# Third attention of a four-layer block: entry rebuilt, rows of the first batch first, differences on GpSimd

## The reference

```
k_raw, v_raw = context @ Wk.T, context @ Wv.T      # keys, values: odd and even columns of the pair
q = rmsnorm(layernorm(x) @ Wq.T)                   # 32 heads of 8, per head
k = rmsnorm(k)                                     # t * rsqrt(mean(t*t) + 1e-6) over the 8
out = softmax(q k / sqrt(8)) v                     # 256 queries, 1601 keys, per batch and head
x = x + out
```

## Time and profile before

| | |
|---|---|
| median of 3 runs | 2695.54 us (2695.38 to 2700.11) |
| the profiled execution | 2690.88 us |
| its span | 2689.1 us |
| TensorE busy, share of the span | 2465.2 us, 92% |
| VectorE | 1728.8 us, 64% |
| ScalarE | 1488.3 us, 55% |
| GpSimd | 1355.9 us, 50% |

### The profile page before, as it was taken

One profiled execution on the slowest core, in us unless ns is written; L12 is line 12 of the kernel. 1 busy time (PEld: TensorE's weight loads), 2 busy tenths in 40 slices (PEclk: granted clock), 3 DMA queues, 4 the chain that ended last, 5 costly groups with the idle time before them and its releaser, 6 DMA issues. The chain is left out here.

```text
span 2689.1 us, 53835 instructions
## 1 busy us (share of the span) xinstructions
PE 2465.2 (92%) x19554; PEld 1718.4 (64%) x19554; DVE 1728.8 (64%) x3372; ACT 1488.3 (55%) x3294; POOL 1355.9 (50%) x917
## 2 busy tenths in 40 slices
PE   6889999979999999999999999999599698989886
PEld 4567777746777777777777777777365343434443
DVE  4345667557877877877877787877213565555446
ACT  2235544445556566556566555565112577777895
POOL 0025655435666766666666666666101375757400
PEclk8889999999999999999999999999699799999999
DMA  4212232230001000010000000003201000000100
GB/s 157 78 54 83 89 94 73 71 123 1 16 17 45 17 17 9 9 45 16 17 17 16 30 17 17 17 1 126 102 10 58 19 20 15 20 15 20 50 4 16
DMA packets 42466, 108.77 MB, mean 40 GB/s; under 512 B 5044, under 2 KB 26040, under 8 KB 37048
## 3 DMA queue, kind: packets, MB, share of 16 engines
q1 hardware_dynamic: 40424, 102.41, 11.3%
q0 software_dynamic: 768, 2.10, 0.2%
q10 hardware_dynamic: 1008, 0.79, 0.1%
HBM read 99.91 MB, written 4.98 MB: 39 GB/s over the span
## 5 line engine op out<-in xcount | busy, mean ns | idle before, releaser
L1212 POOL TENSOR_TENSOR xn<-xn,l_p 128x512 f32<-128x512 f32 (+1 forms) x400 | 634.7, 1587 | 178.0 <-ACT l_p L1254 161.3
L2205 ACT ACTIVATE l_p<-psum 128x1024 f32<-128x1024 f32 x416 | 399.4, 1034 | 101.0 <-PE psum L2334 98.1
L1340 DVE TENSOR_TENSOR l_plo<-l_p,l_phi 128x512 fp32r<-128x512 f32 (+1 forms) x464 | 405.4, 875 | 63.1 <-ACT l_p L1254 41.1
L1253 ACT ACTIVATE l_phi<-psum 128x512 fp32r<-128x512 f32 (+1 forms) x464 | 279.4, 602 | 219.2 <-PE psum L447 139.8
L1389 DVE TENSOR_REDUCE l_mx<-psum 128x1 f32<-128x512 f32 (+2 forms) x512 | 306.2, 618 | 35.8 <-PE psum L1553 35.2
L2182 POOL TENSOR_TENSOR l_rs<-l_ms,half_power 128x32 f32<-128x32 f32 x45 | 247.5, 5500 | 122.8 <-DVE l_ms L2230 122.8
L2347 PE MATMUL psum<-l_p,l_vs 64*32 64x256 f32 x6656 | 260.5, 378 | 26.9 <-issue 21.6
L1254 ACT ACTIVATE l_p<-psum 128x512 f32<-128x512 f32 (+1 forms) x464 | 281.4, 606 | 0.0
L1483 PE MATMUL psum<-l_m,l_ones 128*128 128x512 f32 (+1 forms) x464 | 232.7, 502 | 0.0
L1572 PE MATMUL psum<-l_w,l_ctx 128*128 128x256 f32 (+1 forms) x832 | 217.0, 383 | 10.0 <-ACT l_qa L1271 6.2
L1553 PE MATMUL psum<-l_kThi,l_qThi 128*128 128x512 f32 (+2 forms) x512 | 199.4, 427 | 5.1 <-DVE l_mx L1389 2.3
(11 more groups left out here) (380 smaller groups left out, 5180.2 us busy)
## 6 DMA issues: line engine op xcount, KB each, us to landing
w_stage<-in_L_w_dram SPq DMA_DIRECT2D x76, 384.0 KB, 3.1
l_w<-in_L_w_qkv_dram SPq DMA_DIRECT2D x16, 1024.0 KB, 4.9
l_ct<-in_ctx_tiles_dram SPq DMA_DIRECT2D x52, 128.0 KB
c_T<-in_ctx_T_dram SPq DMA_DIRECT2D x4, 1601.0 KB
l_ctx<-in_ctx_T_dram SPq DMA_DIRECT2D x4, 1601.0 KB, 6.9
c_N<-in_ctx_dram SPq DMA_DIRECT2D x4, 1536.0 KB
s_wg<-in_L_gate_dram SPq DMA_DIRECT2D x4, 1024.0 KB, 11.8
s_wu<-in_L_up_dram SPq DMA_DIRECT2D x4, 1024.0 KB, 13.8
```

What stands on the lines that cost most here:

```text
L1212: g_.tensor_tensor(l2_acc[k][0:r, :], first[0:r, :], l2_p[c % 3][0:r, :], ALU.add)\
L1253: act.activation(l2_phi[c % 3][0:r, :], src, ACT.Exp).then_inc(l2_e, 1)
L1340: v.tensor_tensor(l2_plo[c % 3][0:r, :], l2_p[c % 3][0:r, :], l2_phi[c % 3][0:r, :].bitcast(F32), ALU.subtract)\
L2205: act.activation(l3_p[ring(odd, c)][:, :], psum[:, (c % 2) * 2 * BANK:(c % 2 + 1) * 2 * BANK], ACT.Exp, scale=float(D3) ** -0.5).then_inc( ...
```

## The change

Places. The entry goes through its 15 tiles in the order `ORDER` = key tiles 0 to 8, query tiles 0 and 1, key tiles 9 to 12; p is the place, QUERIES_AT = 9.

GpSimd. The low half's subtraction moves from VectorE to GpSimd (`low`), in the entry alone. Beside the first four of them GpSimd issues the eight gathers, two at a time; they are no longer in `top_pool`. Then come the inverse roots of rows 0 and 1, the other differences, the zeroing of `l3_vs[0]` after place 9, and behind the last difference `l3_vs[1]`, the copy into `l3_vs[0]`, the inverse roots of rows 2 to 7 and the memset of `l3_qT[1]`.

VectorE. Rows 0 and 1 are added and their statistics taken after place 3's pair, they are normalised after place 5's, rows 2 to 7 are added after place 7's. Statistics and normalising of rows 2 to 7 stand in steps 0 and 2 of batch 0, behind all of the entry. The scaled keys have two buffers (`l3_n`, `l3_sq`). TensorE turns rows 0 and 1 after the projection of place 7, ScalarE copies them before place 8's squares. Rows 2 to 7 are turned two at a time by TensorE at steps 5, 8 and 11 of batch 0 (`REST_TURN`), through bank 7, and copied by VectorE.

Copies. The first query tile is turned into bank 6 and copied by ScalarE at place 13, the second into bank 4 and copied by VectorE at the end.

Steps. The turn is at 15 + 6q instead of 14 + 6q, and VectorE's `turned` stands in the next step, behind `gather` and before `add_out` and `squares`. SyncE loads the query weights when the last expert tile is stored, before the loads of key tile 4 and on.

```diff
-            g.wait_ge(s_yland, 16 * TILES2)
-            for n in range(NT):
-                g.indirect_dma_start(s_yg[:, n, :], None, s_out[:, :], bass.IndirectOffsetOnAxis(s_pos[:, n:n + 1], 0))\
-                    .then_inc(s_got, 16)
...
+        def gather_rows(g, first, end):
+            for n in range(first, end):
+                g.indirect_dma_start(s_yg[:, n, :], None, s_out[:, :], bass.IndirectOffsetOnAxis(s_pos[:, n:n + 1], 0))\
+                    .then_inc(s_scat if n < TB else s_got, 16)
...
-        FIRST_HALF, SECOND_HALF, SQUARES, POWER, PAIRS, TURN = (beside(at) for at in (0, 3, 4, 5, 12, 14))
+        FIRST_HALF, SECOND_HALF, SQUARES, POWER, PAIRS, TURN = (beside(at) for at in (0, 3, 4, 5, 12, 15))
...
+        KEY_BANKS, TURN_BANKS, NORM_BANK, QUERY_BANK = (0, 1, 2, 3), (7, 5), 6, 4
+        ORDER = [*range(MC - PT), *range(MC, N3), *range(MC - PT, MC)]
+        QUERIES_AT = ORDER.index(MC)
+        COMBINE_AT, NORM_AT, REST_AT = 3, 5, 7
...
+            def queries(p):
+                act.wait_ge(l3_init, 1)
+                act.wait_ge(l3_T, p + 1)
+                for n in range(HG):
+                    dst, src = query_part(ORDER[p], n)
+                    ins = act.activation(dst, src, ACT.Copy)
+                ins.then_inc(l3_qd, 1)
...
+            for p in range(N3):
+                if p == QUERIES_AT - 1:
+                    act.wait_ge(xT_ps, LN_PS + 1)
+                    for c in range(DC):
+                        act.activation(xT[:, c, 0:S], bank(NORM_BANK, S, c * S), ACT.Copy).then_inc(xT_cp, 1)
+                square(p)
+                if ORDER[p] < MC:
+                    value(p)
+                if p >= 1:
+                    root(p - 1)
+                if p >= PT:
+                    turned(p - PT)
...
+            def pairs(p):
+                v.wait_ge(l3_rsd, p + 1)
+                need(v, l3_pd, p - 1)
+                need(v, l3_T, p - 1)
+                hi, _, norm, both = pair_parts(p)
+                dve_steps.then(v, v.tensor_tensor(norm, l3_heads(source(p)[:, 0:D]),
+                                                  l3_rs[p % PT][:, :].unsqueeze(2).to_broadcast([P, H3, D3]), ALU.mult))
+                v.tensor_copy(hi, both).then_inc(l3_hid, 1)
...
+                if p == COMBINE_AT + 1:
+                    combine(v, 0, TB)
+                    v.wait_ge(x_upd, X_AT[5] + TB)
+                    rows_stats(v, 0, TB)
+                if p == NORM_AT + 1:
+                    rows_norm(v, 0, 0, TB)
+                if p == REST_AT + 1:
+                    combine(v, TB, NT)
+            pairs(N3 - 1)
...
+            def low(p):
+                g.wait_ge(l3_hid, p + 1)
+                hi, lo, _, both = pair_parts(p)
+                g.tensor_tensor(lo, both, hi, ALU.subtract).then_inc(l3_pd, 1)
...
+            low(0)
+            g.wait_ge(s_yland, 16 * TILES2)
+            gather_rows(g, 0, TB)
+            low(1)
+            gather_rows(g, TB, TB + 2)
+            low(2)
+            gather_rows(g, TB + 2, TB + 4)
+            low(3)
+            gather_rows(g, TB + 4, NT)
+            rows_root(g, 0, 0, TB)
+            for p in range(PT, N3):
+                low(p)
+                if p == QUERIES_AT:
+                    ones_at(0)
+            g.wait_ge(x_upd, X_AT[6])
+            ones_at(1)
+            g.wait_ge(l3_kvd, 2 * N3)
+            g.tensor_copy(l3_vs[0][:, :, :, 0:D3], l3_v0[:, :, 0:HG, :]).then_inc(l3_vsd, 1)
+            rows_root(g, 1, TB, NT)
...
+                if p == QUERIES_AT - 2:
+                    pe.wait_ge(s_yd, TILES2)
+                    rows_turn(pe, 0, NORM_BANK)
+                if p >= PT - 1:
+                    turn(p - PT + 1)
...
+                    sp.wait_ge(s_yland, 16 * TILES2)
+                    sp.dma_start(l3_wq[:, :, :], t["L3_q"]).then_inc(l3_wland, 16)
...
+                if b == 0 and s == 0:
+                    v.wait_ge(x_upd, X_AT[6])
+                    rows_stats(v, TB, NT)
+                if b == 0 and s == OUT_AT + 1:
+                    v.wait_ge(l3_init, 2)
+                if b == 0 and s == OUT_AT:
+                    rows_norm(v, 1, TB, NT)
+                if b == 0 and s in REST_TURN:
+                    part = REST_TURN.index(s) + 1
+                    v.wait_ge(xT_ps, LN_PS + part + 1)
+                    v.tensor_copy(xT[:, :, part * S:(part + 1) * S], bank(7).rearrange("p (c m) -> p c m", c=DC)).then_inc(xT_cp, 1)
...
                 if j == 0 and done[0] >= 0:
                     gather(*done)
+                if new is not None and s - 1 in TURN:
+                    turned(new, TURN[s - 1])
...
-                    if s in TURN:
-                        turned(new, TURN[s])
...
+                    pe.wait_ge(xT_cp, LN_CP + DC + part - 1)
+                    rows_turn(pe, part, 7)
```

More of the change, by code:

```diff
@@ L2037, in first_scalar, with square @@
-            norm_scalar(act, ln_l3x)
-            for t in range(MC, N3):
-                square(t)
-            for t in range(MC, N3):
-                root(t)
-            act.wait_ge(l3_init, 1)
-            act.wait_ge(l3_T, N3 - 1)
-            for n in range(HG):
-                dst, src = query_part(N3 - 2, n)
-                ins = act.activation(dst, src, ACT.Copy)
-            ins.then_inc(l3_Td, 1)
+            def square(p):
+                query = ORDER[p] >= MC
+                act.wait_ge(l3_kv, QUERIES_AT + TB if query else p + 1)
+                need(act, l3_msd, p - PT + 1)
+                act.activation(l3_raw[p % PT][:, :], source(p)[:, 0:D], ACT.Square).then_inc(l3_kvd, 2 if query else 1)
@@ L2048, in first_scalar, with mean @@
+            root(N3 - 1)
+            for p in range(N3 - PT, N3):
+                turned(p)
             act.preload_act_table(ACT.Exp)
         def first_vector(v):
-            def mean(t):
-                v.wait_ge(l3_kvd, 2 * t + (1 if t < MC else 2))
-                need(v, l3_rsd, t - PT + 1)
-                ms = l3_ms[t % PT][:, :]
-                dve_steps.then(v, v.tensor_reduce(ms, l3_heads(l3_raw[t % PT][:, :]), AX.X, ALU.add))
+            def mean(p):
+                v.wait_ge(l3_kvd, 2 * p + (2 if ORDER[p] >= MC else 1))
+                need(v, l3_rsd, p - PT + 1)
+                ms = l3_ms[p % PT][:, :]
+                dve_steps.then(v, v.tensor_reduce(ms, l3_heads(l3_raw[p % PT][:, :]), AX.X, ALU.add))
@@ new lines, in first_vector @@
+            for p in range(N3):
+                mean(p)
+                if p >= 1:
+                    pairs(p - 1)
+                if p == COMBINE_AT + 1:
[7 more added lines that the diff above has]
+            pairs(N3 - 1)
+            last = QUERIES_AT + 1
@@ L2085, in first_vector, with pair_parts @@
             v.wait_ge(l3_init, 1)
-            v.wait_ge(l3_T, N3)
+            v.wait_ge(l3_T, last + 1)
             for n in range(HG):
-                dst, src = query_part(N3 - 1, n)
+                dst, src = query_part(ORDER[last], n)
                 ins = v.tensor_copy(dst, src)
-            ins.then_inc(l3_Td, 1)
-        def first_pool(g):
-            g.wait_ge(x_upd, X_AT[6])
-            norm_pool(g, ln_l3x)
-            for n in range(2):
+            ins.then_inc(l3_qd, 1)
+        def pair_parts(p):
+            norm = l3_heads((l3_n, l3_sq)[p % 2][:, :])
+            both = norm.unsqueeze(2).to_broadcast([P, H3, 2, D3])
+            dst = l3_pairs[p % 2]
+            if ORDER[p] < MC:
+                return dst[:, :, 0::2, :], dst[:, :, 1::2, :], norm, both
+            return dst[:, :, 0:2, :], dst[:, :, 2:4, :], norm, both
```

179 lines of the change are left out of this document (87 added, 92 removed).

## The result

| | before | after |
|---|---|---|
| median of the runs (us) | 2696.72 (4 runs) | 2676.97 (4 runs, 2674.06 to 2678.91) |
| ratio, 95% interval | | 0.9924, 0.9909 to 0.9938 |
| profiled execution, span | 2690.88, 2689.1 | 2677.45, 2675.6 |
| start of the entry (first key projection) | 2059.66 | 2066.95 |
| entry, to the first scores | 69.99 | 55.22 |

The account below looks back on a forecast made before the run. VectorE was taken as busiest in the 70.0 us entry to the third attention, TensorE as deciding in the steps. -10.4 + 1.3 + 2.3 = -6.8 us: 2684.1 profiled, 2688.7 against the median; range 2680 to 2699.

Parts of the forecast that it names:

- largest term: Entry to the third attention, first key projection to first scores: 59.6 us instead of 70.0, -10.4.
- ordinary turns: Ten turns a batch moved beside the second projection half: +0.14 us each, 1.4 a batch.
- part 5: Steps, turn moved from 14 + 6q to 15 + 6q: +0.75 us a batch, +2.3 over three batches.
- part 3: End of the entry: first scores 11.1 us after T, place 12's point, forecast at 2108.2; so at 2119.3.
- Part 1: Entry up to tile 6: GpSimd's difference holds VectorE's tensor_scalar, GpSimd sets the pace; tile 6's half at 2086.6.
- second rival: Entry: the engines do not exclude each other, TensorE's 2.17 to 2.2 us sets the pace; -11.8, 2683.7; chance 0.15.
- Part 2: Entry, places 7 to 12: six pieces at 2.75 us, six additions, zeroing; sum 21.6, place 12 at 2108.2.
- Part 4: First batch's steps: rows 2 to 7 finished there, TensorE's three turns of two rows cost +1.3 us.
- five special turns: Moved turns in the steps: step 15 +1.05 us, step 38's -0.6, step 80 -0.85, step 93 -1.2, last +0.95.
- The low clock: Rival, entry: four tiles at TensorE's low clock cost about 5 us; 2693.7, no change; chance 0.12.
- The slow difference: Rival, entry: GpSimd's differences from place 4 become the bound; at 2.6 us each +15.6, 2704; chance 0.10.
- the costly turns: Rival, steps: turns cost more than counted, 13 us at worst, half likely; 2695, no change; chance 0.10.

Follow-up runs that it names:

- after_2: The kernel after, unchanged, measured once more: entry 56.21 us, steps 436.81, ratio to before 0.9941.
- s_both: The kernel before with only the steps' part: turn at 15 + 6q, its copy behind the next step's gather. Steps 432.12 us, ratio to before 0.9969.
- no_scalar: The kernel after without VectorE's tensor_scalar of the mean; ScalarE's square root takes its scale and epsilon. Entry 53.63 us, ratio to before 0.9933.
- table: The kernel after with the exponential's table load ahead of ScalarE's last two key copies. Entry 55.22 us, ratio to before 0.9939.
- q_late: The kernel after with ScalarE's first query block copies behind the key copies of places 11 and 12. Entry 56.65 us, ratio to before 0.9933.
- all_v: The kernel after with all differences on VectorE, no tensor_scalar of the mean, query copies on VectorE, earlier table load. Entry 54.58 us, ratio to before 0.9939.
- all_gp: The kernel after with places 0 to 3's differences and query copies on VectorE, no tensor_scalar of the mean, earlier table load. Entry 49.17 us, ratio to before 0.9910.
- all_gp_2: Repeat of all_gp, unchanged: entry 49.92 us, median 2670.97, ratio to before 0.9913.
- s_ordinary: The kernel before with only the ten ordinary turns of a batch moved to 15 + 6q, copies behind the next gather. Steps 440.06 us, ratio to before 1.0003.
- d_all: The kernel after with all fifteen of the entry's differences back on VectorE. Entry 53.70 us, ratio to before 0.9922.
- s_copy: The kernel before with only the turn's copy moved behind the next step's gather. Steps 439.03 us, ratio to before 0.9998.
- e_only: The kernel after with the steps' turn at 14 + 6q and its copy as before. Entry 56.18 us, steps 443.22, ratio to before 0.9956.

## Why the forecast was wrong

Its sign and its largest term were right; the sum was 13 us short, 4.4 in the entry (3.4 by after_2) and 9.7 in the steps, less 1.2 for the rows. Two steps of the sum failed in the main: the ordinary turns of part 5, which had the wrong sign (7.3 us), and ScalarE's query copies of part 3 (2.8 us).

**Part 1 gave the right number, by luck.** Forecast for the half of place 6: 26.9 us after the start; measured to its end 27.1. The difference takes 1.15 (1.3 taken), and what it does to VectorE is what the step says. The Trainium skill (SBUF — State Buffer, Who interferes with whom) states that a tensor_scalar in a two-port mode and a GpSimd instruction exclude each other and that the later one waits for the whole of the other. This trace agrees: the tensor_scalar beside the difference takes 0.91 instead of 0.18. The second rival, no exclusion, is out. But the way to 27.1 is another one. GpSimd's root of two rows ends 21.1 us after the start and not 23.8, because differences and gathers follow each other at 3.57 instead of 3.93 and the root stands behind four differences where I counted five. What it gains is lost again in what I did not count: a cast that takes 1.74 beside a difference, the normalising at 1.55 for 0.96, and 1.29 us in which VectorE waits for TensorE, which turns the two rows first.

**Part 2, "a tile costs 2.75", was mis-sized: 2.40.** Of the 0.35, 0.15 are the difference, 0.07 the wait ahead of it (0.08 for 0.15), and 0.13 the way from its end to the end of the next cast, 1.17 instead of 1.31. The zeroing costs what was said: 3.82 between two casts against 2.40. The six additions cost 2.5 instead of 3.7, and 1.4 come in that were not in the sum: place 7's squares wait for TensorE, which projects that tile at the low clock (3.77 from cast to cast). From place 6 to 12: 19.8 us, not 21.6.

**Part 3, "scores at T + 11.1", was the entry's largest error: T + 8.3.** I let ScalarE begin its query copies at T. In its queue they stand behind the root of place 12, and VectorE forms that place's mean a whole place ahead of its cast: they begin at 2110.89, 3.0 us before T (2113.85). So they hold the mean of place 14 for 1.55 us only, and the last half ends at T + 4.8 instead of 7.3.

**Part 4 was right in its term and incomplete.** Three turns cost 1.4 (1.3). But the first batch got 2.5 longer: the exponential's table load behind ScalarE's last key copy (0.56) was in no step. I had moved these copies to ScalarE in my sum and not asked what stood behind them in its queue. Nor had I asked what VectorE's copies of the rows stand in front of: the one of step 11 makes the first gather 0.36 late. The last 0.2 are the low clock.

**Part 5 had the wrong sign, and it was the ordinary turns.** For each term, a middle batch of s_both against before, by the starts of the values' matmuls step by step:

| turns | forecast | measured |
|---|---|---|
| ten ordinary | +1.4 | -1.0 |
| step 15 | +1.05 | +0.75 |
| step 39 | -0.6 | -0.66 |
| step 80 | -0.85 | -0.91 |
| step 93 | -1.2 | -1.4 |
| last turn, next batch's first scores | +0.95 | +1.0 |
| sum | +0.75 | -2.2 |

The five special turns came out near their terms. The step that failed is "a turn in that step costs +0.14": it took a turn alone for partly hidden under a wait (0.42) and a turn beside a projection for full (0.56). Measured are 0.42 alone and 0.41 beside, and four of the ten turns gave back more than that where they left. That is 2.4 us a batch and 7.3 of the 9.7. The special ones give 1.6; 0.8 are left, 0.1 in the first batch and 0.7 at the beginning of the fourth, where no turn was moved. The rows of the waits do not show this: from before to s_both they fall by 2.9 us (35.5 to 32.6, without that of the first scores) where the steps get 7.4 shorter, because a part of a wait that lies between overlapping instructions is in no row.

**The rivals.** The low clock did come: for 3.4 us at place 7 (6.8 in after_2), which cost 0.8 (1.8) in that tile, and again from 2118.4 on; not for four tiles. The slow difference and the costly turns did not.

What stays open: why the fourth batch begins 0.7 us shorter; why the clock falls behind a wait in one trace and stays at 1.00 behind the same wait in another; and what puts the entry's start 8 us apart. The clock has a part in the last: ahead of the entry it was low for 143.4 us in all in after, no_scalar, after_2 and table, which start at 2063.9 to 2067.0, and for 126.3 in before and q_late, which start at 2059.7 and 2058.7; but s_both, with 122.9, starts at 2061.8.

## What to carry to other kernels

Before work goes to a neighbouring engine, look at which of the old engine's instructions will have to wait for the new one: here the move paid nothing while one 0.18 us tensor_scalar stood against it, and some 4 to 5 us once its scale and bias were put into the square root (all_v against all_gp and all_gp_2, with the reservations above). When an instruction changes its place, write out each queue as it will then stand, what is ahead and what is behind (a table load, a copy). Do not price a move within a step by a difference of overlaps such as 0.14 us times thirty; move it alone and measure, or carry it with both signs. And look at the granted clock of each stretch before two traces are subtracted: s_ordinary as a whole said that nothing had changed, where 1.0 us had been gained a batch and 0.9 lost to the clock.

## What was not expected of the hardware

A reciprocal, a reduce and a product with one operand in the accumulators ran at their 0.35, 0.41 and 0.42 us beside GpSimd's subtraction, where tensor_scalar and casts were held: 2.33 us for one that met a difference and then a 128x1664 memset. GpSimd's subtraction of 128x512 with f16 as one input and as output took 1.15, no more than the 1.29 of the earlier trace rows. Eight gathers in a row on GpSimd (0.94 each) held no cast in d_all (0.46 and 0.47). Yet in after a tensor_scalar of 0.17 that starts beside a gather (2083.03, the gather ends at 2083.62) ends only with the difference behind that gather, after 1.81. A wait of 2.2 us at step 93 was followed by the low clock in s_copy and s_ordinary, in all three batches, and in none of before and e_only, which have the same wait; one of 1.8 us at step 65 in five of eighteen traces, in one batch each. And kernels whose entry and steps are alike differ by up to 8 us ahead of the change from one execution to the next.
